# The end of a graph layer on one core: the last four row tiles as two rounds of two through the same ring memory

## The chip, the core and the metric

The kernel runs on one core of a Trainium2 chip. The metric is the device time of one execution in microseconds (us). Matmuls run on PE (TensorE), copies and square roots on ACT (ScalarE), everything elementwise on DVE (VectorE). SP (SyncE) only issues DMAs; ACT issues three small ones.

## What is computed

One layer of a graph network with residual and layer norm, all in float32, with x of 8192 x 64, adj of 8192 x 8192 (268 MB, stored dense), w of 8192 and W of 64 x 64:

```python
agg = adj @ (x @ W_agg)
y = x + w[:, None] * relu(agg) + (1.0 - w)[:, None] * x
out = (y - mean(y)) / sqrt(var(y) + 1e-5)      # over the 64 columns
```

## The kernel before

The 8192 rows of the output are 64 row tiles of 128 rows. The kernel computes (adj @ x) @ W, so that W comes in only at the end of each group of tiles. For one group of n tiles it contracts over 64 blocks of 128 rows of x: block j is `x_sb[:, j]` (128 x 64) as the stationary operand and 128 x (n·128) numbers of the transposed matrix as the moving one. Even blocks add up in PSUM partitions 0 to 63, odd ones in 64 to 127. The host has laid the matrix out so that a load of some blocks is one run of memory per partition.

There are 15 main groups of four tiles (512 columns), then a group of three ("mid", 384 columns) and a group of one ("last", 128 columns). Each main group comes in three loads of 22, 22 and 20 blocks (5.77, 5.77 and 5.24 MB), which go to the three slots of `ring`. The mid group comes in eight loads (`MID_LOADS`), the last group in nine (`LAST_LOADS`); mid starts at the beginning of `ring`, last lies behind it, in the third slot.

SP issues all loads on one queue, in the order of the program. A main load waits on `slot_free` until PE has consumed what stood in its slot three loads ago (L119 to L123). The mid loads wait for as many slots as they reach into (L126 to L132), the last loads for the third slot (L133). After them SP waits until 63 tiles are done and stores them (2 MB, L140 and L141); ACT stores the last tile (L214).

PE (L167 to L187) waits for each load on the load's own semaphore and contracts it (`contract`, L156). When a group is complete, ACT copies the sums from PSUM to `aggT` (L203, L208, L211) and PE turns them back (`turn_back`, L164): one matmul per tile, with `aggT` stationary and W, stacked twice, moving, which also adds the even and odd halves. Then DVE does the rest: `weigh` (L245) and `normalise` (L234 to L242) for the groups of four and three tiles, with ACT's square root (L199) in between. The group of one tile has a shorter chain of its own with `bn_stats` and `bn_aggr` (L261 to L267). Each DVE step waits for the one before it. A program's matmul in fp32 appears in the profile as two MATMULs, so 22 blocks are 44 of them.

Of the kernel before, what the change touches and what calls it, by code (L numbers as in the profile page):

```python
# [4 lines left out]
P = 128  # L5
D = 64
EPS = 1e-5
HALVES = 1
MAIN_SLOTS = 4
MID_SLOTS = 3  # L10
LAST_SLOTS = 1
SUB = 64
MAIN_LOADS = (22, 22, 20)
MID_LOADS = (16, 12, 12, 8, 8, 4, 2, 2)
LAST_LOADS = (10, 12, 12, 10, 7, 5, 4, 2, 2)


def gnn_residual_layernorm(nc, x, adj_main, adj_mid, adj_last, w, w_agg, out):

# [10 lines left out]
    ALU = mybir.AluOpType  # L30
# [2 lines left out]

    T = x.shape[0] // P
    G = adj_main.shape[0]
    MID, LAST = G, G + 1
    MID_T0 = G * MAIN_SLOTS
    LAST_T0 = MID_T0 + MID_SLOTS
    COLS, MID_COLS = MAIN_SLOTS * P, MID_SLOTS * P
    C = len(MAIN_LOADS)  # L40
    SLOT = max(MAIN_LOADS) * COLS
    LAST_AT = T * MID_COLS
    assert SUB == T == sum(MAIN_LOADS) == sum(MID_LOADS) == sum(LAST_LOADS) and LAST_T0 + LAST_SLOTS == T
    assert LAST_AT + T * P <= C * SLOT and LAST_AT > (C - 1) * SLOT


    DVE_PRE = 2
    DVE_GROUP, VAR_STEP = 7, 6
    LAST_STEP0 = DVE_PRE + LAST * DVE_GROUP
    LAST_VAR_STEP = 4  # L50

    ctx = ExitStack()
    with ctx:
        def sb(name, shape):
            return ctx.enter_context(nc.sbuf_tensor(name, shape, fp32))
# [4 lines left out]
        def sem(name):  # L60
            return ctx.enter_context(nc.semaphore(name))
# [5 lines left out]
        two_minus_w = sb("two_minus_w", [P, T])  # L67
        wagg2 = sb("wagg2", [P, D])
        eps = sb("eps", [P, 1])
        aggT = sb("aggT", [P, COLS])  # L70
        y = sb("y", [P, MAIN_SLOTS, D])
        sq = sb("sq", [P, MAIN_SLOTS, D])
# [1 line left out]
        varsum = sb("varsum", [P, MAIN_SLOTS])  # L74
        std = sb("std", [P, MAIN_SLOTS])
        rstd = sb("rstd", [P, MAIN_SLOTS])
        y_last = sb("y_last", [P, D])
        rstd_last = sb("rstd_last", [P, 1])
        std_last = sb("std_last", [P, 1])
        stats = sb("stats", [P, 6])  # L80
        mv = sb("mv", [P, 2])

        bank = psum("bank", [P, 8, 512])
        acc = bank[:, 0]
        mid_acc = bank[:, 1, 0:MID_COLS]
        last_acc = bank[:, 2, 0:P]
        rows_ps = bank[:, 3, 0:MAIN_SLOTS * D]
        mid_rows = bank[:, 4, 0:MID_SLOTS * D]
        last_rows = bank[:, 5, 0:D]

        loaded = [sem(f"loaded{c}") for c in range(C)]
        mid_loaded = [sem(f"mid_loaded{k}") for k in range(len(MID_LOADS))]
        last_loaded = [sem(f"last_loaded{k}") for k in range(len(LAST_LOADS))]
# [3 lines left out]
        mid_done, last_done = sem("mid_done"), sem("last_done")  # L97
        agg_copied = sem("agg_copied")
        rows_done = sem("rows_done")
        dve_step = sem("dve_step")  # L100
# [6 lines left out]
        @block.sync  # L107
        def _(sp):
            sp.dma_start(x_sb[:], x.rearrange("(p t) d -> p t d", p=P)).then_inc(x_in, 16)  # L109
            sp.dma_start(w_sb[:], w.rearrange("(p t) -> p t", p=P)).then_inc(w_in, 16)  # L110
            def main_load(c, load):

                j, n = sum(MAIN_LOADS[:c]), MAIN_LOADS[c]
                sp.dma_start(ring[:, c * SLOT:c * SLOT + n * COLS], load[:, :, j:j + n].rearrange("o q s n -> (o q) (s n)")  # L114
                             ).then_inc(loaded[c], 16)

            for c in range(C):
                main_load(c, adj_main[0:1, 0])
            with sp.Fori(1, G) as g:  # L119
                for c in range(C):  # L120

                    sp.wait_ge(slot_free, g * C + (c + 1 - C))
                    main_load(c, adj_main[bass.ds(g, 1), 0])  # L123

            j, freed = 0, 0
            for k, n in enumerate(MID_LOADS):  # L126
                while freed * SLOT < (j + n) * MID_COLS:
                    freed += 1
                    sp.wait_ge(slot_free, (G - 1) * C + freed)
                sp.dma_start(ring[:, j * MID_COLS:(j + n) * MID_COLS],  # L130
                             adj_mid[0, :, j:j + n].rearrange("q s n -> q (s n)")).then_inc(mid_loaded[k], 16)
                j += n  # L132
            sp.wait_ge(slot_free, G * C)  # L133
            j = 0
            for k, n in enumerate(LAST_LOADS):
                sp.dma_start(ring[:, LAST_AT + j * P:LAST_AT + (j + n) * P],
                             adj_last[:, j:j + n].rearrange("q s n -> q (s n)")).then_inc(last_loaded[k], 16)
                j += n

            sp.wait_ge(out_ready, LAST)  # L140
            sp.dma_start(out_rows[:, 0:LAST_T0], res[:, 0:LAST_T0]).then_inc(stored, 16)  # L141

        @block.gpsimd
        def _(pool):
            nc.gpsimd.memset(eps[:], EPS).then_inc(eps_ready, 1)

        @block.tensor
        def _(pe):
            pe.wait_ge(x_in, 16)
            pe.wait_ge(wagg_in, 32)  # L150

            def contract(into, at, cols, j0, n):

                for s in range(n):
                    j = j0 + s
                    last = nc.tensor.matmul(into[j % 2 * D:(j % 2 + 1) * D, 0:cols], x_sb[:, j],  # L156
                                            ring[:, at + s * cols:at + (s + 1) * cols], start=j < 2, stop=j >= T - 2)
                return last

            def turn_back(rows, n, copied):  # L160

                pe.wait_ge(agg_copied, copied)
                for i in range(n):
                    last = nc.tensor.matmul(rows[:, i * D:(i + 1) * D], aggT[:, i * P:(i + 1) * P], wagg2[:], start=True, stop=True)  # L164
                last.then_inc(rows_done, 1)

            with pe.Fori(0, G) as g:  # L167
                for c in range(C):
                    pe.wait_ge(loaded[c], g * 16 + 16)
                    contract(acc, c * SLOT, COLS, sum(MAIN_LOADS[:c]), MAIN_LOADS[c]).then_inc(slot_free, 1)  # L170

                pe.wait_ge(dve_step, g * DVE_GROUP + DVE_PRE)
                turn_back(rows_ps, MAIN_SLOTS, g + 1)
            j = 0
            for k, n in enumerate(MID_LOADS):
                pe.wait_ge(mid_loaded[k], 16)
                last = contract(mid_acc, j * MID_COLS, MID_COLS, j, n)
                j += n
            last.then_inc(mid_done, 1)
            turn_back(mid_rows, MID_SLOTS, MID + 1)  # L180
            j = 0
            for k, n in enumerate(LAST_LOADS):
                pe.wait_ge(last_loaded[k], 16)
                last = contract(last_acc, LAST_AT + j * P, P, j, n)
                j += n
            last.then_inc(last_done, 1)
            turn_back(last_rows, LAST_SLOTS, LAST + 1)  # L187

        @block.scalar
        def _(act):  # L190
# [10 lines left out]
            with act.Fori(0, G) as g:  # L201
# [5 lines left out]
            act.wait_ge(mid_done, 1)  # L207
            nc.scalar.copy(aggT[:, 0:MID_COLS], mid_acc).then_inc(agg_copied, 1)  # L208
            std_of(std[:, 0:MID_SLOTS], varsum[:, 0:MID_SLOTS], 1.0 / D, MID * DVE_GROUP + (DVE_PRE + VAR_STEP))
            act.wait_ge(last_done, 1)  # L210
            nc.scalar.copy(aggT[:, 0:P], last_acc).then_inc(agg_copied, 1)  # L211
            std_of(std_last[:], mv[:, 1:2], 1.0, LAST_STEP0 + LAST_VAR_STEP)
# [5 lines left out]
        def _(dve):  # L218
            def step(instruction, count):
                instruction.then_inc(dve_step, 1)  # L220
                dve.wait_ge(dve_step, count)
# [32 lines left out]
            base = MID * DVE_GROUP + DVE_PRE  # L254
            dve.wait_ge(rows_done, MID + 1)
            weigh(mid_rows, MID_T0, MID_SLOTS, base)
            normalise(MID, MID_T0, MID_SLOTS, base)

            v, t = y_last[:], LAST_T0
            dve.wait_ge(rows_done, LAST + 1)  # L260
            step(nc.vector.tensor_scalar(v, last_rows, 0.0, w_sb[:, t:t + 1], ALU.max, ALU.mult), LAST_STEP0 + 1)  # L261
            step(nc.vector.tensor_tensor(v, v, res[:, t], ALU.add), LAST_STEP0 + 2)  # L262
            step(nc.vector.bn_stats(stats[:], v), LAST_STEP0 + 3)  # L263
            step(nc.vector.bn_aggr(mv[:], stats[:]), LAST_STEP0 + LAST_VAR_STEP)  # L264
            dve.wait_ge(std_ready, LAST + 1)
            step(nc.vector.reciprocal(rstd_last[:], std_last[:]), LAST_STEP0 + 5)
            nc.vector.tensor_scalar(res[:, t], v, mv[:, 0:1], rstd_last[:, 0:1], ALU.subtract, ALU.mult).then_inc(out_ready, 1)  # L267


# [31 lines left out]
```

## Time and profile before

| | |
|---|---|
| three runs | 638.78, 640.0, 640.12 us, median 640.0 |
| the profiled execution | 638.89 us, its span in the trace 637.0 us |
| mean granted clock of TensorE | 0.912 of full speed |
| bytes moved by DMA | 272.75 MB, mean 428 GB/s |
| busy | PE 82%, DVE 9%, ACT 2% of the span |

The span is what the trace covers; the time of the execution is 1.9 us longer. Times in the trace count from the start of the span.

### The profile page before, as it was taken

The page shows a single profiled execution, that of the slowest core. Times are in us where ns is not written, and L with a number is a line of the kernel's source. Part 1 is how long each engine was busy: PE and PEld are TensorE (multiplying, and loading weights), DVE is VectorE, ACT ScalarE, POOL GpSimd, SP SyncE. Part 2 cuts the span into 40 slices and gives each one's busy share as a digit, 9 for nine tenths or more (in the row PEclk, how much of TensorE's full clock was granted, in tenths as well). Part 3 has the DMA queues.
Part 4 walks back from the last instruction along what each step waited for, and adds up shares of the span by engine and source line. Part 5 has one row for each costly group of instructions (what it writes and reads, how often), then busy time and mean ns, then how long its engine had stood idle before and what let it go on. Part 6 is the DMA issues. An engine that isn't in the chain of part 4 may idle for free.

```text
span 637.0 us, 5371 instructions
## 1 busy us (share of the span) xinstructions
PE 519.5 (82%) x2304; PEld 177.2 (28%) x2304; DVE 55.8 (9%) x136; ACT 15.9 (2%) x35; POOL 0.3 (0%) x5
## 2 busy tenths in 40 slices
PE   0678798878987888797878977878887987978996
PEld 0123232222222322222222322322222222222345
DVE  2000101010010100101001010100101001010102
ACT  0000000000000000000000000000000000000000
POOL 0000000000000000000000000000000000000000
PEclk9997898888979889897988979898888989888999
DMA  9999999999999999999999999999999999999998
GB/s 362 453 418 453 419 427 433 425 447 428 444 414 447 419 429 443 441 432 419 451 410 436 436 450 423 427 431 425 446 424 453 424 429 419 436 444 420 428 413 349
DMA packets 9667, 272.75 MB, mean 428 GB/s; under 512 B 1472, under 2 KB 1728, under 8 KB 3008
## 3 DMA queue, kind: packets, MB, share of 16 engines
q1 hardware_dynamic: 9360, 272.63, 99.6%
q10 hardware_dynamic: 304, 0.07, 0.1%
q8 instruction: 3, 0.05, 0.0%
HBM read 270.60 MB, written 2.10 MB: 428 GB/s over the span
## 4 chain that ended last, share of the span: by engine, by line
DMA 69%; PE 29%; issue 0%; SPq 0%; ACT 0%; DVE 0%; DVEq 0%
DMA ring<-adj_main_dram 69%; PE bank L156 29%; PE bank L164 0%; SPq L114 0%; ACT aggT L203 0%; ACT aggT L208 0%; SPq L110 0%; SPq L109 0%; DVE res L267 0%; ACT std_last L199 0%; DVE y_last L261 0%; ACT aggT L211 0%; DVE stats L263 0%; DVE y_last L262 0%; DVE mv L264 0%
## 5 line engine op out<-in xcount | busy, mean ns | idle before, releaser
L156 PE MATMUL bank<-ring,x_sb 128*64 128x512 f32 (+2 forms) x2176 | 501.7, 621 | 102.2 <-DMA ring<-adj_main_dram 102.1
L156 PEld LDWEIGHTS bank<-ring,x_sb 128*64 128x64 f32 x2176 | 161.6, 148 | 430.2 <-issue 299.7
L245 DVE SCALAR_TENSOR_TENSOR y<-bank,w_sb 128x256 f32<-128x256 f32 (+1 forms) x16 | 6.7, 420 | 552.7 <-PE bank L164 552.7
L164 PE MATMUL bank<-wagg,aggT 128*128 128x64 f32 x128 | 17.9, 281 | 11.2 <-ACT aggT L203 10.3
L164 PEld LDWEIGHTS bank<-wagg,aggT 128*128 128x128 f32 x128 | 15.6, 191 | 25.4 <-ACT aggT L203 23.5
L203 ACT COPY aggT<-bank 128x512 f32<-128x512 f32 x15 | 8.8, 585 | 527.0 <-PE bank L156 527.0
L234 DVE TENSOR_TENSOR y<-y,res 128x256 f32<-128x256 f32 (+1 forms) x16 | 6.7, 420 | 2.2
L242 DVE TENSOR_TENSOR res<-y,rstd 128x256 f32 (+1 forms) x16 | 6.7, 421 | 0.6
L238 DVE TENSOR_TENSOR sq<-y 128x256 f32<-128x256 f32 (+1 forms) x16 | 6.7, 421 | 0.6
L236 DVE SCALAR_TENSOR_TENSOR y<-rowsum,y 128x256 f32<-128x256 f32 (+1 forms) x16 | 6.7, 420 | 0.5
L239 DVE TENSOR_REDUCE varsum<-sq 128x4 f32<-128x256 f32 (+1 forms) x16 | 6.7, 416 | 0.5
L235 DVE TENSOR_REDUCE rowsum<-y 128x4 f32<-128x256 f32 (+1 forms) x16 | 6.6, 416 | 0.6
L199 ACT ACTIVATE std<-varsum,eps 128x4 f32<-128x4 f32 (+1 forms) x16 | 4.8, 297 | 65.7 <-DVE varsum L239 65.7
L230 DVE TENSOR_TENSOR res<-x_sb,two_minus_w 128x4096 f32<-128x4096 f32 x1 | 4.4, 4425 | 0.0
L241 DVE RECIPROCAL rstd<-std 128x4 f32<-128x4 f32 (+1 forms) x16 | 2.8, 178 | 6.9 <-ACT std L199 6.9
L194 ACT ACT_TABLE_LOAD x1 | 1.3, 1283 | 2.0 <-issue 2.0
L227 DVE TENSOR_SCALAR two_minus_w<-w_sb 128x64 f32<-128x64 f32 x1 | 0.2, 194 | 9.2 <-DMA w_sb<-w_dram 9.2
L208 ACT COPY aggT<-bank 128x384 f32<-128x384 f32 x1 | 0.5, 478 | 17.5 <-PE bank L156 17.5
L261 DVE TENSOR_SCALAR y_last<-bank,w_sb 128x64 f32<-128x64 f32 x1 | 0.3, 284 | 4.8 <-PE bank L164 4.8
L211 ACT COPY aggT<-bank 128x128 f32<-128x128 f32 x1 | 0.3, 265 | 4.7 <-PE bank L156 4.7
L199 ACT ACTIVATE std_last<-mv,eps 128x1 f32<-128x1 f32 x1 | 0.3, 296 | 1.6 <-DVE mv L264 1.6
L267 DVE TENSOR_SCALAR res<-y_last,mv,rstd_last 128x64 f32<-128x64 f32 x1 | 0.3, 314 | 0.0
(9 smaller groups left out, 1.3 us busy)
## 6 DMA issues: line engine op xcount, KB each, us to landing
ring<-adj_main_dram SPq DMA_DIRECT2D x30, 5632.0 KB, 27.2
ring<-adj_main_dram SPq DMA_DIRECT2D x15, 5120.0 KB, 29.8
ring<-adj_mid_dram SPq DMA_DIRECT2D x2, 2304.0 KB, 22.8
ring<-adj_mid_dram SPq DMA_DIRECT2D x1, 3072.0 KB, 21.5
ring<-adj_mid_dram SPq DMA_DIRECT2D x2, 1536.0 KB, 23.9
x_sb<-x_dram SPq DMA_DIRECT2D x1, 2048.0 KB, 8.0
out_dram<-res SPq DMA_DIRECT2D x1, 2016.0 KB, 8.1
ring<-adj_last_dram SPq DMA_DIRECT2D x2, 768.0 KB, 23.0
```

What stands on the lines that cost most here:

```text
L156: last = nc.tensor.matmul(into[j % 2 * D:(j % 2 + 1) * D, 0:cols], x_sb[:, j], ring[:, at + s * cols:at + (s + 1) * cols], start=j < 2, st ...
L164: last = nc.tensor.matmul(rows[:, i * D:(i + 1) * D], aggT[:, i * P:(i + 1) * P], wagg2[:], start=True, stop=True)
L199: nc.scalar.activation(out_std, var, ACT.Sqrt, bias=eps[:, 0:1], scale=scale).then_inc(std_ready, 1)
L203: nc.scalar.copy(aggT[:], acc).then_inc(agg_copied, 1)
L230: step(nc.vector.tensor_tensor(res[:], x_sb[:], over_row(two_minus_w[:]), ALU.mult), DVE_PRE)
L234: step(nc.vector.tensor_tensor(v, v, residual, ALU.add), base + 2)
L235: step(nc.vector.tensor_reduce(rowsum[:, 0:n], v, AX.X, ALU.add), base + 3)
L236: step(nc.vector.scalar_tensor_tensor(out=v, in0=over_row(rowsum[:, 0:n]), scalar=-1.0 / D, in1=v, op0=ALU.mult, op1=ALU.add), base + 4)
L238: step(nc.vector.tensor_tensor(s, v, v, ALU.mult), base + 5)
L239: step(nc.vector.tensor_reduce(varsum[:, 0:n], s, AX.X, ALU.add), base + VAR_STEP)
L242: nc.vector.tensor_tensor(residual, v, over_row(rstd[:, 0:n]), ALU.mult).then_inc(out_ready, 1)
L245: step(nc.vector.scalar_tensor_tensor(out=y[:, 0:n], in0=rows.rearrange("p (n d) -> p n d", d=D), scalar=0.0, in1=over_row(w_sb[:, bass.ds ...
```

## The change

The last four tiles become two groups of two ("pairs", 256 columns each), and both go through one loop body.

- The host arrays keep their names: `adj_mid` now holds tiles 60 and 61, `adj_last` tiles 62 and 63.
- A pair comes in seven loads of 20, 15, 11, 8, 5, 3 and 2 blocks. Both rounds use the same place, the first 64 x 256 columns of `ring`, which reach into the second slot. Load k of round one waits for the slots, load k of round two for `pair_free` to reach k + 1, which PE counts up behind each contracted piece.
- PE runs both rounds in one `Fori(0, 2)`. ACT copies a pair tile by tile, and each matmul of turning back waits for its own copy.
- DVE runs `weigh` and `normalise` on two tiles in both rounds; the shorter chain for one tile is gone. Before each round DVE waits for `out_ready` of its previous group.
- The last load (20 blocks) of the last main group is issued as two of 10. PE waits for the second half on `rest_loaded` in all 15 passes, at a value from a register: 1 in the first 14 (a memset on POOL counts it up at the start) and 17 in the last.
- The first store now covers 62 tiles, the second two tiles (64 KB).

```diff
+PAIR_LOADS = (20, 15, 11, 8, 5, 3, 2)
+REST = 10
...
-            with sp.Fori(1, G) as g:
+            with sp.Fori(1, G - 1) as g:
...
+            for c in range(C):
+                sp.wait_ge(slot_free, (G - 1) * C + (c + 1 - C))
+                whole = MAIN_LOADS[c] - (REST if c == C - 1 else 0)
+                main_load(c, adj_main[G - 1:G, 0], 0, whole, loaded[c])
+            main_load(C - 1, adj_main[G - 1:G, 0], whole, whole + REST, rest_loaded)
+            def pair_load(k, group):
+                j, n = sum(PAIR_LOADS[:k]), PAIR_LOADS[k]
+                sp.dma_start(ring[:, j * PAIR_COLS:(j + n) * PAIR_COLS], group[:, j:j + n].rearrange("q s n -> q (s n)")
+                             ).then_inc(pair_loaded[k], 16)
+            freed = 0
+            for k in range(K):
+                while freed * SLOT < sum(PAIR_LOADS[:k + 1]) * PAIR_COLS:
                     freed += 1
                     sp.wait_ge(slot_free, (G - 1) * C + freed)
+                pair_load(k, adj_mid[0])
+            for k in range(K):
+                sp.wait_ge(pair_free, k + 1)
+                pair_load(k, adj_last)
...
+                    if c < C - 1:
+                        last = contract(acc, c * SLOT, COLS, j, n)
+                    else:
+                        whole = n - REST
+                        contract(acc, c * SLOT, COLS, j, whole)
+                        pe.wait_ge(rest_loaded, (g + (16 - (G - 1))) // 16 * 16 + 1)
+                        last = contract(acc, c * SLOT + whole * COLS, COLS, j + whole, REST)
+                    last.then_inc(slot_free, 1)
...
+            with pe.Fori(0, 2) as r:
+                j = 0
+                for k, n in enumerate(PAIR_LOADS):
+                    pe.wait_ge(pair_loaded[k], r * 16 + 16)
+                    contract(pair_acc, j * PAIR_COLS, PAIR_COLS, j, n).then_inc(pair_free, 1)
+                    j += n
+                for i in range(PAIR):
+                    pe.wait_ge(agg_copied, r * PAIR + (G + i + 1))
+                    last = nc.tensor.matmul(pair_rows[:, i * D:(i + 1) * D], aggT[:, i * P:(i + 1) * P], wagg2[:], start=True, stop=True)
+                last.then_inc(rows_done, 1)
...
+            for r in range(2):
+                act.wait_ge(pair_free, (r + 1) * K)
+                for i in range(PAIR):
+                    nc.scalar.copy(aggT[:, i * P:(i + 1) * P], pair_acc[:, i * P:(i + 1) * P]).then_inc(agg_copied, 1)
+                std_of(std[:, 0:PAIR], varsum[:, 0:PAIR], 1.0 / D, (G + r) * DVE_GROUP + (DVE_PRE + VAR_STEP))
...
+            for r in range(2):
+                base, t0 = (G + r) * DVE_GROUP + DVE_PRE, PAIR_T0 + r * PAIR
+                dve.wait_ge(out_ready, G + r)
+                dve.wait_ge(rows_done, G + r + 1)
+                weigh(pair_rows, t0, PAIR, base)
+                normalise(G + r, t0, PAIR, base)
```

SP's queue behind the last main load, before the change (the sizes are numbers per partition; 384 columns of a mid block, 128 of a last one):

```order
L130 DMA ring<-adj_mid_dram 128x768 x2
L136 DMA ring<-adj_last_dram 128x1280 [waits slot_free]
L136 DMA ring<-adj_last_dram 128x1536 x2
L136 DMA ring<-adj_last_dram 128x1280
L136 DMA ring<-adj_last_dram 128x896
L136 DMA ring<-adj_last_dram 128x640
L136 DMA ring<-adj_last_dram 128x512
L136 DMA ring<-adj_last_dram 128x256 x2
L141 DMA out_dram<-res 128x4032 [waits out_ready]
```

The loads of the last group wait once, for a slot. The same place after the change:

```order
L126 DMA ring<-adj_mid_dram 128x512
L126 DMA ring<-adj_last_dram 128x5120 [waits pair_free]
L126 DMA ring<-adj_last_dram 128x3840 [waits pair_free]
L126 DMA ring<-adj_last_dram 128x2816 [waits pair_free]
L126 DMA ring<-adj_last_dram 128x2048 [waits pair_free]
L126 DMA ring<-adj_last_dram 128x1280 [waits pair_free]
L126 DMA ring<-adj_last_dram 128x768 [waits pair_free]
L126 DMA ring<-adj_last_dram 128x512 [waits pair_free]
L142 DMA out_dram<-res 128x3968 [waits out_ready]
```

Every load of the second round now waits for PE, and the big store stands behind all of them as before.

DVE at the end of the program, before the change: the group of three tiles, then the chain of the single tile.

```order
L242 TENSOR_TENSOR res<-y,rstd 128x192
L261 TENSOR_SCALAR y_last<-bank,w_sb 128x64
L262 TENSOR_TENSOR y_last<-y_last,res 128x64
L263 BN_STATS stats<-y_last 128x6
L264 BN_AGGR mv<-stats 128x2
L266 RECIPROCAL rstd_last<-std_last 128x1
L267 TENSOR_SCALAR res<-y_last,mv,rstd_last 128x64
```

And after it, the end of round one and round two:

```order
L250 TENSOR_TENSOR res<-y,rstd 128x128
L253 SCALAR_TENSOR_TENSOR y<-bank,w_sb 128x128
L242 TENSOR_TENSOR y<-y,res 128x128
L243 TENSOR_REDUCE rowsum<-y 128x2
L244 SCALAR_TENSOR_TENSOR y<-rowsum,y 128x128
L246 TENSOR_TENSOR sq<-y 128x128
L247 TENSOR_REDUCE varsum<-sq 128x2
L249 RECIPROCAL rstd<-std 128x2
L250 TENSOR_TENSOR res<-y,rstd 128x128
```

Six operations on 64 numbers per partition have become eight, on 128.

## Rows read from the trace of the kernel before

**Rows 1.** The page: span, and busy tenths of PE and the DMA engines.
```profile
span 637.0 us, 5371 instructions
PE 519.5 (82%) x2304; PEld 177.2 (28%) x2304; DVE 55.8 (9%) x136; ACT 15.9 (2%) x35; POOL 0.3 (0%) x5
DMA  9999999999999999999999999999999999999998
```
**Rows 2.** The page: the chain of work that ended last, by engine.
```profile
DMA 69%; PE 29%; issue 0%; SPq 0%; ACT 0%; DVE 0%; DVEq 0%
```
**Rows 3.** Timeline: start us, us, engine line op out<-in xcount [idle before <-releaser].
```profile
579.82 11.36 PE L156 MATMUL bank<-ring,x_sb 128*64 128x512 f32 x44 [2.12 <-DMA ring<-adj_main_dram]
...
591.95 8.80 PE L156 MATMUL bank<-ring,x_sb 128*64 128x512 f32 x40 [0.77 <-DMA ring<-adj_main_dram]
...
602.48 20.86 PE L156 MATMUL bank<-ring,x_sb 128*64 128x384 f32 x128
```
**Rows 4.** SP's last issues in the timeline, and the same by size and us to landing.
```profile
601.64 0.43 SPq L130 DMA_DIRECT2D ring<-adj_mid_dram  x1
ring<-adj_mid_dram SPq DMA_DIRECT2D x1, 384.0 KB, 19.8
617.46 0.79 SPq L136 DMA_DIRECT2D ring<-adj_last_dram  x1
ring<-adj_last_dram SPq DMA_DIRECT2D x1, 128.0 KB, 14.1
628.18 0.34 SPq L141 DMA_DIRECT2D out_dram<-res  x1
out_dram<-res SPq DMA_DIRECT2D x1, 2016.0 KB, 8.1
```
**Rows 5.** Timeline of the end; the final row is ACT's store in the list of DMA issues.
```profile
624.73 7.38 PE L156 MATMUL bank<-ring,x_sb 128*64 128x128 f32 x128
632.16 0.27 ACT L211 COPY aggT<-bank 128x128 f32<-128x128 f32 x1 [4.68 <-PE bank L156]
632.95 0.28 DVE L261 TENSOR_SCALAR y_last<-bank,w_sb 128x64 f32<-128x64 f32 x1 [4.80 <-PE bank L164]
634.61 0.31 DVE L267 TENSOR_SCALAR res<-y_last,mv,rstd_last 128x64 f32<-128x64 f32 x1
634.95 0.35 ACTq L214 DMA_DIRECT2D out_dram<-res  x1
out_dram<-res ACTq DMA_DIRECT2D x1, 32.0 KB, 1.7
```
**Rows 6.** Stretches: us, busy (xcount) of PE, PEld, DVE, ACT, POOL; PEclk, DMA share, GB/s.
```profile
566.49:569.90 3.41, 3.41 (x10) 1.09 (x12) 0.83 (x3) 0.30 (x1) 0.00 (x0) 0.54 0.98 423
633.50:634.50 1.00, 0.00 (x0) 0.00 (x0) 0.51 (x3) 0.30 (x1) 0.00 (x0) 1.00 0.50 210
634.50:635.50 1.00, 0.00 (x0) 0.00 (x0) 0.38 (x2) 0.00 (x0) 0.00 (x0) 0.50 0.23 97
631.55:637.00 5.45, 1.00 (x14) 0.62 (x8) 1.40 (x6) 0.56 (x2) 0.00 (x0) 0.77 0.53 216
```
**Rows 7.** Timeline of PE: main loads contracted after waits of different length.
```profile
35.36 9.66 PE L156 MATMUL bank<-ring,x_sb 128*64 128x512 f32 x44 [1.25 <-DMA ring<-adj_main_dram]
217.42 11.36 PE L156 MATMUL bank<-ring,x_sb 128*64 128x512 f32 x44 [1.03 <-DMA ring<-adj_main_dram]
463.46 11.36 PE L156 MATMUL bank<-ring,x_sb 128*64 128x512 f32 x44 [1.97 <-DMA ring<-adj_main_dram]
```
**Rows 8.** Mean ns by shape, then the end of the three-tile group in the timeline.
```profile
L242 DVE TENSOR_TENSOR res<-y,rstd 128x256 f32 x15 | 6.4, 425 | 0.5
L242 DVE TENSOR_TENSOR res<-y,rstd 128x192 f32<-128x192 f32 x1 | 0.4, 357 | 0.0
627.18 0.30 ACT L199 ACTIVATE std<-varsum,eps 128x3 f32<-128x3 f32 x1 [3.32 <-DVE varsum L239]
627.58 0.18 DVE L241 RECIPROCAL rstd<-std 128x3 f32<-128x3 f32 x1 [0.43 <-ACT std L199]
627.79 0.36 DVE L242 TENSOR_TENSOR res<-y,rstd 128x192 f32<-128x192 f32 x1
```

More of the change, by code:

```diff
@@ L9 @@
 MAIN_SLOTS = 4
-MID_SLOTS = 3
-LAST_SLOTS = 1
+MID_SLOTS = 2
+LAST_SLOTS = 2
 SUB = 64
 MAIN_LOADS = (22, 22, 20)
-MID_LOADS = (16, 12, 12, 8, 8, 4, 2, 2)
-LAST_LOADS = (10, 12, 12, 10, 7, 5, 4, 2, 2)
+PAIR_LOADS = (20, 15, 11, 8, 5, 3, 2)
+REST = 10
 def gnn_residual_layernorm(nc, x, adj_main, adj_mid, adj_last, w, w_agg, out):
@@ L35, in gnn_residual_layernorm @@
     G = adj_main.shape[0]
[L36 to L39, printed above, removed]
+    LAST = G + 1
+    PAIR = MID_SLOTS
+    PAIR_T0 = G * MAIN_SLOTS
+    LAST_T0 = PAIR_T0 + PAIR
+    COLS, PAIR_COLS = MAIN_SLOTS * P, PAIR * P
     C = len(MAIN_LOADS)
     SLOT = max(MAIN_LOADS) * COLS
-    LAST_AT = T * MID_COLS
-    assert SUB == T == sum(MAIN_LOADS) == sum(MID_LOADS) == sum(LAST_LOADS) and LAST_T0 + LAST_SLOTS == T
-    assert LAST_AT + T * P <= C * SLOT and LAST_AT > (C - 1) * SLOT
+    K = len(PAIR_LOADS)
+    assert G <= 16 and SUB == T == sum(MAIN_LOADS) == sum(PAIR_LOADS) and LAST_T0 + LAST_SLOTS == T and PAIR == LAST_SLOTS
+    assert T * PAIR_COLS <= C * SLOT
     DVE_PRE = 2
     DVE_GROUP, VAR_STEP = 7, 6
-    LAST_STEP0 = DVE_PRE + LAST * DVE_GROUP
-    LAST_VAR_STEP = 4
     ctx = ExitStack()
@@ L69, in gnn_residual_layernorm @@
         eps = sb("eps", [P, 1])
+        one = sb("one", [P, 1])
         aggT = sb("aggT", [P, COLS])
@@ L76, in gnn_residual_layernorm @@
         rstd = sb("rstd", [P, MAIN_SLOTS])
[L77 to L81, printed above, removed]
         bank = psum("bank", [P, 8, 512])
         acc = bank[:, 0]
[L85 to L89, printed above, removed]
+        pair_acc = bank[:, 1, 0:PAIR_COLS]
+        rows_ps = bank[:, 2, 0:MAIN_SLOTS * D]
+        pair_rows = bank[:, 3, 0:PAIR * D]
         loaded = [sem(f"loaded{c}") for c in range(C)]
-        mid_loaded = [sem(f"mid_loaded{k}") for k in range(len(MID_LOADS))]
-        last_loaded = [sem(f"last_loaded{k}") for k in range(len(LAST_LOADS))]
+        rest_loaded = sem("rest_loaded")
+        pair_loaded = [sem(f"pair_loaded{k}") for k in range(K)]
+        pair_free = sem("pair_free")
         slot_free = sem("slot_free")
@@ L96, in gnn_residual_layernorm @@
         eps_ready = sem("eps_ready")
-        mid_done, last_done = sem("mid_done"), sem("last_done")
         agg_copied = sem("agg_copied")
@@ L110, in _, with main_load @@
             sp.dma_start(w_sb[:], w.rearrange("(p t) -> p t", p=P)).then_inc(w_in, 16)
[L111 to L115, printed above, removed]
+            def main_load(c, load, first, end, landed):
+                j, at = sum(MAIN_LOADS[:c]), c * SLOT
+                sp.dma_start(ring[:, at + first * COLS:at + end * COLS],
+                             load[:, :, j + first:j + end].rearrange("o q s n -> (o q) (s n)")).then_inc(landed, 16)
@@ L117, in _ @@
             for c in range(C):
-                main_load(c, adj_main[0:1, 0])
-            with sp.Fori(1, G) as g:
+                main_load(c, adj_main[0:1, 0], 0, MAIN_LOADS[c], loaded[c])
+            with sp.Fori(1, G - 1) as g:
                 for c in range(C):
                     sp.wait_ge(slot_free, g * C + (c + 1 - C))
[L123 to L127, printed above, removed]
+                    main_load(c, adj_main[bass.ds(g, 1), 0], 0, MAIN_LOADS[c], loaded[c])
@@ L128, in _ @@
+            freed = 0
+            for k in range(K):
+                while freed * SLOT < sum(PAIR_LOADS[:k + 1]) * PAIR_COLS:
                     freed += 1
                     sp.wait_ge(slot_free, (G - 1) * C + freed)
[L130 to L138, printed above, removed]
+                pair_load(k, adj_mid[0])
@@ L145, in _ @@
             nc.gpsimd.memset(eps[:], EPS).then_inc(eps_ready, 1)
+            nc.gpsimd.memset(one[:], 1.0).then_inc(rest_loaded, 1)
         @block.tensor
@@ L169, in _ @@
                     pe.wait_ge(loaded[c], g * 16 + 16)
-                    contract(acc, c * SLOT, COLS, sum(MAIN_LOADS[:c]), MAIN_LOADS[c]).then_inc(slot_free, 1)
+                    j, n = sum(MAIN_LOADS[:c]), MAIN_LOADS[c]
+                    if c < C - 1:
[6 more added lines that the diff above has]
+                    last.then_inc(slot_free, 1)
                 pe.wait_ge(dve_step, g * DVE_GROUP + DVE_PRE)
                 turn_back(rows_ps, MAIN_SLOTS, g + 1)
[L174 to L187, printed above, removed]
+            with pe.Fori(0, 2) as r:
[8 more added lines that the diff above has]
+                last.then_inc(rows_done, 1)
         @block.scalar
@@ L206, in _ @@
                 act.wait_ge(out_ready, g + 1)
[L207 to L212, printed above, removed]
+            for r in range(2):
[3 more added lines that the diff above has]
+                std_of(std[:, 0:PAIR], varsum[:, 0:PAIR], 1.0 / D, (G + r) * DVE_GROUP + (DVE_PRE + VAR_STEP))
             act.wait_ge(out_ready, LAST + 1)
@@ L252, in _ @@
                 normalise(g, g * MAIN_SLOTS, MAIN_SLOTS, base)
[L254 to L267, printed above, removed]
+            for r in range(2):
[4 more added lines that the diff above has]
+                normalise(G + r, t0, PAIR, base)
 def kernel(x, adj, L0_gnn_w, L0_gnn_W_agg):
```

## The prediction

> **What bounds the kernel now.** I read the page first, then the DMA issues with their times to landing, then the timeline of the end, and last the stretches. The reader should see in the page that all 16 DMA engines are busy in practically every slice, while PE is busy 82% of the span and every other engine far less [rows 1]. The chain that ended last says the same: 69% of it is a wait for the matrix and 29% is PE consuming it [rows 2]. So the body of the kernel costs what its bytes cost, and the change leaves the bytes alone. Only the end can differ: when does the last load land, and how much work follows it?
>
> The timeline gives the fixed point. The last load of the last main group lands at 591.95, where PE starts on it [rows 3]. Behind it, 16.78 MB of matrix are left (64 blocks x 128 rows x 512 columns x 4 bytes). The last of these loads is issued at 617.46 and lands 14.1 us later, at 631.56 [rows 4]. That is 39.6 us, or 424 GB/s. The 2 MB store is issued at 628.18 and lands 8.1 us later, at 636.3 [rows 4]; that is 4.7 us behind the last load, the time of 2.06 MB at 435 GB/s. So the queue serves in order: the store waits behind the loads and doesn't slow them. After the last landing, PE ends at 632.11, ACT copies, PE turns one tile back, DVE normalises until 634.92, and the final 32 KB store, issued at 634.95, lands 1.7 us later, at 636.65 [rows 5]. Everything after 631.56 is a serial tail of 5.1 us, and it runs with the DMA engines at 53% [rows 6]. The change rebuilds just this tail.
>
> **The change, part by part.**
>
> *The last load of the last main group in halves.* PE finishes the load before it at 591.18 (579.82 + 11.36) and then idles 0.77 until 591.95 [rows 3]. Ten blocks are now there earlier, so PE starts at 591.2 and finishes at about 599.8 instead of 600.75. PE is 0.95 us earlier into the tail groups, at 601.5 instead of 602.48 [rows 3]. That is slack, not time: the loads set the end. In the 15 passes the added wait on a register costs PE some register work beside DMA waits of 0.77 us and more: nothing.
>
> *Bytes and loads.* After 591.95, 17 loads become 14. At 432 GB/s, the pace of the main loads (5.24 MB from 579.82 to 591.95 [rows 3]), 16.78 MB take 38.8 us; the 17 loads took 39.6, so I put 0.045 us on each. Fourteen, and one more main load, save 0.09 us: last landing 631.47.
>
> *Two rounds through one ring memory.* Load k of round two may be issued only when PE has consumed piece k of round one. Is PE in time? One block takes PE 20.86 us / 64 = 0.326 at 384 columns [rows 3] and 7.38 / 64 = 0.115 at 128 [rows 5]; at 256 I take 0.215, two thirds of 0.326 without the drain at its end. PE frees the first piece at 601.5 + 20 x 0.215 = 605.8 and the seventh at 615.4. Round one's loads end at 591.95 + 8.39 MB / 0.425 = 611.7. So the first load of round two (2.6 MB, 6.1 us of work) is queued 5.9 us before the queue would run dry, the other six by 615.4, before that first one has landed at 617.8. The queue never empties. Cost nothing; the cover is those 5.9 us.
>
> *PE at the end.* The pieces of round two land at 617.8, 622.4, 625.8, 628.3, 629.8, 630.8 and 631.47. From the fourth on, 18 blocks x 0.215 = 3.9 us follow 628.35, so PE ends at 632.23 instead of 632.11: +0.12.
>
> *Copy and turning back.* Before: 0.79 us from the start of the copy (632.16) to DVE (632.95) [rows 5]. Now two copies of 128 columns follow each other and the second matmul waits for the second copy. The first matmul is hidden behind the second copy, so one copy of 0.27 and its gap are added: +0.29.
>
> *Normalising two tiles with seven steps in place of one with six.* An operation takes 425 ns on 256 elements and 357 on 192 [rows 8], so about 290 on 128; with the gap of 34 ns of the 192-wide run a step is 0.325. Six steps make 1.95. From the square root to the reciprocal it takes 0.40 (627.18 to 627.58), from there to the last operation 0.21 (to 627.79) [rows 8], and that operation 0.29: 2.85 in all, against 634.92 - 632.95 = 1.97 [rows 5]: +0.88. DVE's new wait for its own previous group is met long before.
>
> *The stores.* The first (62 tiles) is issued near 620 but stands behind all loads, and lands at 636.2, near where it lands now; the second is issued at about 636.2, so the first no longer matters. The last store is 64 KB instead of 32. The trace has no 64 KB store. By the 32 KB one it is 1.7 us [rows 5]; from below I allow 1.4, since the big store has just left the engines, from above 2.2. I take 1.7, the nearest row: 0.
>
> The sum is 0.12 + 0.29 + 0.88 = 1.29; the 0.09 of the earlier landing is already in the 632.23. The profiled execution took 638.89, so it would become 640.2. It lies low among the runs: with the three (638.78, 640.0, 640.12) the mean is 639.4, and the forecast for a median of runs is 640.7.
>
> One rule speaks for the other sign. Loads under 1 MiB: twelve of the last 17 before, six of 14 now. The last 4.19 MB, in nine such loads, came between 621.4 (where the last load of the three-tile group, issued at 601.64, landed after 19.8 us) and 631.56 [rows 4]: 413 GB/s, only 4% under the main loads. The Trainium skill, "DMA: Bandwidth & Descriptors", section Bandwidth, asks for DMAs of at least 1 MiB for 75% of the peak. By that rule the small loads would have been some 2.4 us dearer than the new ones, and the change would be faster by about 1.1 us; the row above disagrees, because loads queued behind each other hide their fixed part here.
>
> **The rivals.**
>
> *PE's clock falls before round two* (35%, slower). After round one PE turns two tiles back (until 616.4) and then waits for the first piece at 617.8, about 1.4 us. Waits of 1.97 us before a main load were followed by the 1.2 GHz level: 11.36 us for 22 blocks; waits of 1.03 to 1.25 us were followed by it three times in eight (11.36 against 9.66 us) [rows 7]. In the 3.4 us after such a wait the mean granted clock was 0.54 [rows 6]. 1.4 us lies between. It would cost 1.7 us on the first piece; PE, with 64 blocks to do in the 13.7 us up to the last landing, couldn't catch up: 617.8 + 1.7 + 13.76 = 633.27, so 1.04 us later. Time 641.7. It decides if the PE clock shows 1.2 GHz after 617.8. For it speaks also that PE has had idle time around the copies; against it, five of eight.
>
> *The leading DMA engines run dry, and the slow ones gain* (9%, faster). After 631.56 the DMA share is 0.50 from 633.5 on and 0.23 from 634.5 [rows 6], though the last store lands only at 636.3. So some engines finish 2 to 3 us before the last, and a landing is set by the slowest. If round two's gate starved the leaders and gave their share to the others, the last load could land up to 2.5 us earlier: 639.4 + 1.3 - 2.5 = 638.2. This needs the leaders, who end round one near 609, to find nothing: but the next load is issued at 605.8, and 1.7 us is what even a whole small store takes to land. So I think it unlikely.
>
> *The gate itself holds the queue* (4%, slower). If PE freed the first piece after 610, a gap would open, and each us adds one: 641.7 with 1 us. The 5.9 us speak against it, even after a slow stretch of 1.7.
>
> *Large loads count for more than I say* (5%, faster). If the price per load grows as its rows shrink, all of the 0.8 us of the 17 loads could vanish, which moves the last landing and all behind it: 639.4 + 1.29 - 0.7 = 640.0. By the rule of the page it would be 1.29 - 2.4 on 639.4, so 638.3.
>
> **How the numbers follow.** The forecast case (47%): full clock, queue full, a tail longer by 1.29 us. Its own range is 0.9 to 1.8 with the bounds of the last store. Timings of this kernel tell a difference of about 0.2%, 1.28 us, from none; so this case is half "same", half "slower". The slow-clock case is slower but for a seventh of it. The two faster cases give 9% faster and the rest same. Together: faster 0.09, same 0.34, slower 0.57. The range takes in the clock case with its spread of runs, (641.7 + 0.8) and below the forecast the spread of the runs, 0.6, and part of the large-load case: 639.2 to 642.7.
>
> **What would show it.** Last load landing within 0.5 us of 631.5; PE's last contraction ending near 632.2 at 2.4 GHz; 1.05 us from there to DVE; DVE's last group 2.85 us; last store issued near 636.2 and the span near 638.3. A DMA share well under 1 between 606 and 631 would show the gate; half clock after 617.8 the first rival; a landing before 631 either of the faster ones. The prediction is wrong if the last load lands over 0.7 us off, since all the rest of the sum hangs on it.

## The result and the profile after

The changed kernel took 641.32 us in the median of 8 runs (640.31 to 642.38), the kernel before 639.92 in 8 (638.69 to 640.17). The ratio is 1.0031 with a 95% interval of 1.0022 to 1.0040: slower by 1.4 to 2.6 us. The two medians differ by 1.40 us, the lower end of that; the runs of both kernels fall into groups, so a median moves with the share of each group. The profiled execution took 640.31, the lowest of the eight, with a span of 638.5; against the 638.89 of the one before that is +1.42.

The page shows the same picture as before [rows 1, 2], with the last slices of the DMA engines a little emptier:

```profile
span 638.5 us, 5392 instructions
PE 519.5 (81%) x2304; PEld 180.8 (28%) x2304; DVE 56.1 (9%) x138; ACT 16.0 (3%) x37; POOL 0.3 (0%) x6
DMA  9999999999999999999999999999999999999997
...
DMA 69%; PE 29%; issue 0%; DVE 0%; SPq 0%; ACT 0%; DVEq 0%
```

The end in the timeline (start us, us, engine line op out<-in xcount [idle before <-releaser]), which answers to [rows 5]; the last row is from the list of DMA issues:

```profile
617.85 14.67 PE L159 MATMUL bank<-ring,x_sb 128*64 128x256 f32 x128 [0.47 <-DMA ring<-adj_last_dram]
632.55 0.43 ACT L219 COPY aggT<-bank 128x128 f32<-128x128 f32 x2 [12.83 <-PE bank L159]
632.87 0.66 PE L195 MATMUL bank<-wagg,aggT 128*128 128x64 f32 x4 [0.35 <-ACT aggT L219]
633.64 0.29 DVE L253 SCALAR_TENSOR_TENSOR y<-bank,w_sb 128x128 f32<-128x128 f32 x1 [13.33 <-PE bank L195]
...
635.58 0.30 ACT L208 ACTIVATE std<-varsum,eps 128x2 f32<-128x2 f32 x1 [2.60 <-DVE varsum L247]
...
636.18 0.29 DVE L250 TENSOR_TENSOR res<-y,rstd 128x128 f32<-128x128 f32 x1
636.50 0.35 ACTq L222 DMA_DIRECT2D out_dram<-res  x1
...
out_dram<-res ACTq DMA_DIRECT2D x1, 64.0 KB, 1.6
```

The reader should see one thread from PE to the last store without a hole: PE ends at 632.52 (617.85 + 14.67), DVE starts 1.09 us after the start of the copies, works 2.83 us, and the store is issued at 636.50 and lands at 638.1.

The gate of round two, in SP's issues, and the landing of loads and of the big store, which answer to [rows 4]. Above the list of issues stands the stretch 634 to 635 (us, busy of PE, PEld, DVE, ACT, POOL, PEclk, DMA share, GB/s), which answers to [rows 6]:

```profile
606.89 9.89 SPq L126 DMA_DIRECT2D ring<-adj_last_dram  x7
620.34 0.34 SPq L142 DMA_DIRECT2D out_dram<-res  x1
...
634.00:635.00 1.00, 0.00 (x0) 0.00 (x0) 0.90 (x4) 0.00 (x0) 0.00 (x0) 1.00 0.08 32
...
ring<-adj_last_dram SPq DMA_DIRECT2D x1, 2560.0 KB, 10.9
out_dram<-res SPq DMA_DIRECT2D x1, 1984.0 KB, 15.8
...
ring<-adj_last_dram SPq DMA_DIRECT2D x1, 256.0 KB, 15.0
```

The first load of round two is issued at 606.89 and lands at 617.8. The last one is issued within 0.1 us of 616.4 and lands 15.0 us later, at 631.4: where the last load landed before (631.56). The big store lands at 636.1. Before, it ended 0.3 us ahead of the last store, so the tail cost little beyond the DMA work that had to be done anyway; now the engines are at 8% in the stretch from 634 to 635, where before the change they were at 50% from 633.5 and at 23% from 634.5 [rows 6], and the end of the tail stands almost alone.

### The profile page after: what moved, and what is told of

It is laid out like the page before. It is cut to its first block, busy times and chain, and to the rows that moved or that the text cites. A ratio compares the mean times of both kernels' runs of the same rounds, so it can differ in the third digit from the quotient of the medians.

```text
span 638.5 us, 5392 instructions
## 1 busy us (share of the span) xinstructions
PE 519.5 (81%) x2304; PEld 180.8 (28%) x2304; DVE 56.1 (9%) x138; ACT 16.0 (3%) x37; POOL 0.3 (0%) x6
## 4 chain that ended last, share of the span: by engine, by line
DMA 69%; PE 29%; issue 0%; DVE 0%; SPq 0%; ACT 0%; DVEq 0%
DMA ring<-adj_main_dram 67%; PE bank L159 29%; DMA ring<-adj_last_dram 2%; SPq L109 0%; PE bank L167 0%; PE bank L195 0%; ACT aggT L212 0%; SPq L105 0%; SPq L104 0%; ACT std L208 0%; DVE sq L246 0%; DVE y L242 0%; DVE y L244 0%; DVE y L253 0%; DVE varsum L247 0%
## 5 line engine op out<-in xcount | busy, mean ns | idle before, releaser
L159 PE MATMUL bank<-ring,x_sb 128*64 128x512 f32 (+1 forms) x2176 | 501.7, 621 | 103.0 <-DMA ring<-adj_main_dram 102.5
L159 PEld LDWEIGHTS bank<-ring,x_sb 128*64 128x64 f32 x2176 | 165.3, 148 | 427.4 <-issue 289.0
```

## The experiments

My theory: the longer serial tail behind an unchanged last landing is the cost in the profiled execution (1.42 us), and what the median has on top is PE's clock, which falls in some executions before round two. Against it stand the gate on PE's consumption, a later landing, and PE's backlog.

The runs of the kernel before that were taken beside the experiments are 29, 23, 21 and 1. They lie in two groups, 638.4 to 639.05 and 639.4 to 640.3, half of them (37 of 74) in the upper one. The medians of the first three sets are 639.46, 638.97 and 638.95, though the groups stay where they are: the median falls into one group or the other. So the runs of a changed kernel are best compared with the groups, and ratios of different sets with care.

### Round two in memory of its own

```diff
-                sp.dma_start(ring[:, j * PAIR_COLS:(j + n) * PAIR_COLS], ...
+                sp.dma_start(ring[:, (r * T + j) * PAIR_COLS:(r * T + j + n) * PAIR_COLS], ...
...
+            sp.wait_ge(slot_free, G * C)
             for k in range(K):
-                sp.wait_ge(pair_free, k + 1)
-                pair_load(k, adj_last)
+                pair_load(k, adj_last, 1)
...
-            with pe.Fori(0, 2) as r:
+            for r in range(2):
```

> The changed kernel, with round two of the pairs in ring memory of its own and both rounds written out, so that no load waits for PE within the pairs. If the longer work behind the last landing is the whole cost (my theory): the same as the changed kernel, 641.3 (ratio to before 1.002 to 1.003), last landing near 631.5. If the gate on PE's consumption holds the queue or skews the DMA engines: the last load lands earlier by what it cost, so 640.0 or less. If it helped (leading engines held back), the last load lands later and the time rises over 642.

Measured: median 642.15 of 6 runs (640.18 to 642.50), ratio 1.0033 (1.0020 to 1.0046). Without the gate it isn't faster. The profiled execution was one of the longer ones (642.37). SP issued its last load at 605.90, 10 us earlier than with the gate, and it landed at the same time:

```profile
605.90 1.16 SPq L126 DMA_DIRECT2D ring<-adj_last_dram  x1
...
ring<-adj_last_dram SPq DMA_DIRECT2D x1, 256.0 KB, 25.6
```

605.90 + 25.6 = 631.5. In the stretches of this trace the DMA engines are busy throughout (0.96 and 0.99 of the time from 617.95 to 624). So neither the gate nor the early end of some DMA engines moves the last landing. What did move is PE:

```profile
614.00 0.66 PE L194 MATMUL bank<-wagg,aggT 128*128 128x64 f32 x4 [0.36 <-ACT aggT L218]
617.95 16.59 PE L158 MATMUL bank<-ring,x_sb 128*64 128x256 f32 x128 [3.29 <-DMA ring<-adj_last_dram]
...
617.95:621.40 3.45, 3.45 (x16) 1.95 (x18) 0.00 (x0) 0.00 (x0) 0.00 (x0) 0.50 0.96 408
```

PE had waited 3.29 us before round two, ran at first at 0.50 of its clock, that is 1.2 GHz, and took 16.59 us for it instead of 14.67.

### The last main load whole again

```diff
-                whole = MAIN_LOADS[c] - (REST if c == C - 1 else 0)
-                main_load(c, adj_main[G - 1:G, 0], 0, whole, loaded[c])
-            main_load(C - 1, adj_main[G - 1:G, 0], whole, whole + REST, rest_loaded)
+                main_load(c, adj_main[G - 1:G, 0], 0, MAIN_LOADS[c], loaded[c])
...
+                    contract(acc, c * SLOT, COLS, j, n).then_inc(slot_free, 1)
```

> The changed kernel with the last load of the last main group whole again. My theory: this load is not on the path once round two starts by its landing (617.8), so the same within 0.3 us of the changed kernel. Rival, PE's backlog: PE starts round one up to 1 us later, frees round two's pieces later and ends later, up to 1 us slower. Second rival, PE's clock: with less waiting before round two (under 0.5 us) there is no fall to 1.2 GHz, and runs that had it lose their tail: faster by up to 1 us in the median.

Measured: median 641.03 of 12 runs, ratio 1.0031 (1.0019 to 1.0043). By the median this is the first reading, 0.29 us from the 641.32 of the changed kernel. But the runs are spread otherwise: two clean groups, six between 639.90 and 640.26, six between 641.79 and 642.85, where the changed kernel had one of eight in the lower group and most between 641.1 and 641.5. The profiled execution (640.13) is of the lower one:

```profile
591.75 8.80 PE L157 MATMUL bank<-ring,x_sb 128*64 128x512 f32 x40 [0.77 <-DMA ring<-adj_main_dram]
617.67 14.67 PE L157 MATMUL bank<-ring,x_sb 128*64 128x256 f32 x128 [0.34 <-DMA ring<-adj_last_dram]
```

With the load whole, PE starts on it only when all of it has landed, at 591.75, takes 8.80 us at full clock, and so has but 0.34 us left to wait before round two. A run in which PE comes later has less still. So the upper group of this kernel can't be a fall of the clock after a long wait before round two; PE coming late, after a fall in the last main load or in round one, would fit, and no trace shows it. So the half load seems to take one kind of longer run away and to bring another, which is argued and not shown.

### The kernel before with the seven-step chain

```diff
-            step(nc.vector.tensor_scalar(v, last_rows, 0.0, w_sb[:, t:t + 1], ALU.max, ALU.mult), LAST_STEP0 + 1)
...
+            weigh(last_rows, LAST_T0, LAST_SLOTS, base)
+            normalise(LAST, LAST_T0, LAST_SLOTS, base)
```

> The kernel before, with the last single tile normalised by the general seven steps in place of the shorter chain. At 64 elements a step is 0.224 + 0.034 us: 6 x 0.258 + 0.40 + 0.21 + 0.22 = 2.4 us against 1.97: if the chain behind the last landing is on the path, slower by 0.4 us (ratio 1.0007). If the big store or the last landing on the slow DMA engines sets the end, 0.

Measured: median 639.09 of 11 runs, ratio 1.0002 (0.9993 to 1.0011). By the medians this is inconclusive: 0.4 us is less than the distance between the two groups of runs. Group by group both lie higher: the seven lower runs have a median of 638.99 for 638.81 in the kernel before, the four upper ones 640.35 for 639.95. The chain in the profile:

```profile
633.10 0.23 DVE L245 SCALAR_TENSOR_TENSOR y<-bank,w_sb 128x64 f32<-128x64 f32 x1 [5.02 <-PE bank L164]
635.24 0.23 DVE L242 TENSOR_TENSOR res<-y,rstd 128x64 f32<-128x64 f32 x1
```

It goes from 633.10 to 635.47, 2.37 us for the 1.97 of before, and the span is 637.4 for 637.0.

### The kernel before with the split main load

```diff
+            for c in range(C):
+                sp.wait_ge(slot_free, (G - 1) * C + (c + 1 - C))
+                whole = MAIN_LOADS[c] - (REST if c == C - 1 else 0)
+                main_load(c, adj_main[G - 1:G, 0], 0, whole, loaded[c])
+            main_load(C - 1, adj_main[G - 1:G, 0], whole, whole + REST, rest_loaded)
...
+                        pe.wait_ge(rest_loaded, (g + (16 - (G - 1))) // 16 * 16 + 1)
+                        last = contract(acc, c * SLOT + whole * COLS, COLS, j + whole, REST)
```

> The kernel before, with the last load of the last main group in two halves and nothing else. There PE works without a pause from 624.73 to 632.11 and ends 0.56 us behind the last landing. If PE's backlog is part of its end: PE ends within 0.25 us of the landing, so 0.3 us faster in the profile, and more in the runs near 640.0, which may be those in which PE's clock fell in the last main group: median 638.9. If the landing alone sets the end: the same as before, median 639.9.

Measured: median 638.82 of 11 runs, all between 638.62 and 639.19; ratio 0.9988 (0.9980 to 0.9997). This is faster than the changed kernel, and against the kernel before it is faster by having no upper group: its median is that of the lower group (638.81). The group near 640 is gone. But the mechanism that I gave for the profile is wrong: PE ended at 632.22, not earlier than before, 0.54 us behind the last landing (617.48 + 14.2 = 631.68). The timeline shows why this isn't backlog: PE now has waits in the mid group.

```profile
579.47 18.25 PE L166 MATMUL bank<-ring,x_sb 128*64 128x512 f32 x84 [3.66 <-DMA ring<-adj_main_dram]
...
599.43 9.25 PE L166 MATMUL bank<-ring,x_sb 128*64 128x384 f32 x56
609.97 6.67 PE L166 MATMUL bank<-ring,x_sb 128*64 128x384 f32 x40 [1.29 <-DMA ring<-adj_mid_dram]
...
632.27 0.27 ACT L230 COPY aggT<-bank 128x128 f32<-128x128 f32 x1 [4.98 <-PE bank L166]
```

PE comes 3 us earlier to the mid group than in [rows 3]: some 0.8 us because it needn't wait for the whole last load, and 1.9 because its clock didn't fall in this execution (18.25 us for the 42 blocks that took 11.36 + 8.80 there). It could have ended earlier if its own work had held it; it follows the loads, half a microsecond behind. That the upper group of the kernel before is PE coming late after a fall of its clock in the last main group fits with this, and was not seen in a trace.

### Filling PE's wait before round two

```diff
                 last.then_inc(rows_done, 1)
+                for f in range(6):
+                    nc.tensor.matmul(bank[f % 2 * D:(f % 2 + 1) * D, 4, 0:PAIR_COLS], x_sb[:, f],
+                                     x_sb[:, 0:4].rearrange("p t d -> p (t d)"), start=True, stop=True)
```

> The changed kernel, with PE contracting 6 blocks (256 columns, 1.3 us) of x with itself into an unused PSUM bank behind each turning back of a pair; nobody reads them. Clock theory: the runs over 641 are those in which PE waited 1 to 3.3 us before round two and then ran at 1.2 GHz. With half or more of that wait filled, most of them go: median 640.2 to 640.8. Rival, the spread comes from the landing of the loads or from elsewhere: 641.0 to 641.4 and two groups of runs as before. Cost of the filler where the wait was only 0.5 us: up to 0.3 us, since PE catches up on the loads.

> The same with 12 blocks (2.6 us). Clock theory: no run of the slow group is left, all within 0.5 us of one another; PE starts round two up to 2.1 us after the first landing in the runs in which it had waited least, which costs these up to 1 us; median 640.3 to 641.2. Rival as in the run with 6: two groups, distance 2 us.

Measured, with 6: median 640.27 of 11 runs, all between 640.12 and 640.55, ratio 1.0018 (1.0009 to 1.0027). With 12: median 640.42 of 12 runs (640.06 to 640.86, and one of 641.83), ratio 1.0020 (1.0011 to 1.0028). Work that nobody reads makes the changed kernel faster by about 1 us in the median (641.32 without it) and, with 6 blocks, takes away every run over 640.6. With 12 blocks "all within 0.5 us" did not come true: the runs spread over 0.8 us, and the one of 641.83 has no trace. The timeline with 6 blocks:

```profile
614.59 1.51 PE L198 MATMUL bank<-x_sb 128*64 128x256 f32 x12
617.78 14.68 PE L159 MATMUL bank<-ring,x_sb 128*64 128x256 f32 x128 [1.68 <-DMA ring<-adj_last_dram]
```

PE turned the first pair back at the same time as in the run with its own memory (614.00 in both), which had 3.29 us to wait and lost its clock; with 1.68 us left to wait it kept it. The price of filling too much shows with 12:

```profile
616.43 2.81 PE L198 MATMUL bank<-x_sb 128*64 128x256 f32 x24
619.07 13.98 PE L159 MATMUL bank<-ring,x_sb 128*64 128x256 f32 x128
```

PE worked on the filling until it started round two at 619.07, 1.3 us after the first load, and ended at 633.05; that run took 640.86.

### Two steps less behind the last landing

On top of the kernel with 6 filling blocks:

```diff
+                if short:
+                    base -= 2
+                else:
                     step(nc.vector.tensor_tensor(v, v, residual, ALU.add), base + 2)
                     step(nc.vector.tensor_reduce(rowsum[:, 0:n], v, AX.X, ALU.add), base + 3)
...
+                normalise(G + r, t0, PAIR, base, short=r == 1)
```

> The kernel with 6 filling blocks (640.27), and in the second round of the pairs DVE leaves out two of its steps: adding the residual, and the row sum (so tiles 62 and 63 lack the residual and use the row sums of tiles 60 and 61). If the serial work behind the last landing sets the end: faster by two steps of 0.324 us, 0.65 us, median 639.6. If the big store on the slow DMA engines or the last landing set it by now (they end near 636.1 in the trace, 2 us before the last store): less than 0.3.

Measured: median 639.58 of 11 runs (639.34 to 639.91), 0.69 us under the same kernel with both steps (640.27), where 0.65 was expected. The two groups of eleven runs don't overlap. Serial work behind the last landing goes into the time in full, although the big store is still under way for part of it.

### One copy in place of two

```diff
-                for i in range(PAIR):
-                    nc.scalar.copy(aggT[:, i * P:(i + 1) * P], pair_acc[:, i * P:(i + 1) * P]).then_inc(agg_copied, 1)
+                nc.scalar.copy(aggT[:, 0:PAIR_COLS], pair_acc).then_inc(agg_copied, PAIR)
```

> The kernel with 6 filling blocks, with one copy of 256 columns in place of two of 128. The two overlap in the trace (0.43 us together) and the first matmul hides behind the second copy. One copy of 256 columns should take 0.37 us (0.27 for 128, 0.48 for 384, 0.59 for 512), and both of PE's turns then follow it, 0.22 us more behind the copy: from the start of the copy to DVE 1.09 + (0.37 - 0.43) + 0.1 = 1.1 to 1.2. Time the same, 640.3 within 0.15. My forecast had counted the second copy at its full 0.27; if the copies didn't overlap, one copy would be 0.15 faster.

Measured: median 640.42 of 11 runs (ten between 640.22 and 640.56, one of 1031.67, which is out of line with all others); no difference beyond the 0.15 us that was allowed for. The copies as one, in the timeline:

```profile
632.53 0.37 ACT L221 COPY aggT<-bank 128x256 f32<-128x256 f32 x1 [13.64 <-PE bank L159]
632.95 0.66 PE L195 MATMUL bank<-wagg,aggT 128*128 128x64 f32 x4 [0.52 <-ACT aggT L221]
633.72 0.29 DVE L255 SCALAR_TENSOR_TENSOR y<-bank,w_sb 128x128 f32<-128x128 f32 x1 [14.24 <-PE bank L195]
```

1.19 us from copy to DVE, for 1.09 with two copies: in the traces, copying tile by tile is worth 0.1 us, and the times (640.42 for 640.27) don't contradict it.

### More executions of the two kernels as they are

> The changed kernel unchanged, for one more profiled execution (the one there is took 640.31; most runs took 641.1 to 641.5). If this one lies over 641: clock theory, PE's wait before round two is over 0.5 us, a stretch of 3.4 us at the start of round two is at 1.2 GHz in part or whole, and PE ends 0.5 to 2 us later than 632.5 with the last landing still at 631.5. Rival: the last landing itself is later.

> The changed kernel once more, for a second profiled execution, with the two readings of the look before: either PE's clock at the start of round two, or a later last landing.

> The kernel before unchanged, once more profiled (its runs lie in two groups, near 638.7 and near 639.9). If it is one near 639.9: by my theory PE's clock falls at the second or third load of the last main group, PE comes to the mid group over 0.5 us later than 602.48, works without a pause and ends 1 us later than 632.11, with the last landing at 631.5. Rival: the last landing is later. If it is one near 638.7 it says nothing.

Measured: 642.48, 640.10 and, for the kernel before, 638.84. The first two are the same program. The longer one, in the timeline and in the stretches from the start of round two on:

```profile
614.11 0.66 PE L195 MATMUL bank<-wagg,aggT 128*128 128x64 f32 x4 [0.36 <-ACT aggT L219]
617.93 16.74 PE L159 MATMUL bank<-ring,x_sb 128*64 128x256 f32 x128 [3.16 <-DMA ring<-adj_last_dram]
...
617.98:621.40 3.42, 3.42 (x17) 1.90 (x19) 0.00 (x0) 0.00 (x0) 0.00 (x0) 0.50 0.96 409
621.40:624.00 2.60, 2.60 (x18) 1.53 (x16) 0.00 (x0) 0.00 (x0) 0.00 (x0) 0.60 1.00 421
...
613.79 0.40 SPq L126 DMA_DIRECT2D ring<-adj_last_dram  x1
ring<-adj_last_dram SPq DMA_DIRECT2D x1, 256.0 KB, 17.7
```

and the shorter one:

```profile
615.47 0.66 PE L195 MATMUL bank<-wagg,aggT 128*128 128x64 f32 x4 [0.37 <-ACT aggT L219]
617.64 14.67 PE L159 MATMUL bank<-ring,x_sb 128*64 128x256 f32 x128 [1.52 <-DMA ring<-adj_last_dram]
```

The last load of the longer one lands at 613.79 + 17.7 = 631.5, as in the profiled execution (631.4). PE waits 3.16 us, contracts round two at half clock at first, and the copies begin at 634.72 instead of 632.35. That is 2.37 us, and the times differ by 2.38. The kernel before fell into its lower group again, so its upper one stays without a trace.

Why the wait differs shows one step earlier. PE's last 42 blocks of the last main group, in the profiled execution of the result, in the shorter one here and in the longer one:

```profile
579.76 20.83 PE L159 MATMUL bank<-ring,x_sb 128*64 128x512 f32 x84 [3.67 <-DMA ring<-adj_main_dram]
579.55 19.80 PE L159 MATMUL bank<-ring,x_sb 128*64 128x512 f32 x84 [2.28 <-DMA ring<-adj_main_dram]
579.75 18.25 PE L159 MATMUL bank<-ring,x_sb 128*64 128x512 f32 x84 [0.79 <-DMA ring<-adj_main_dram]
```

18.25 us is the time at full clock. Where the clock fell here, PE came later to the pairs and had little to wait before round two (0.47 and 1.52 us); where it didn't, PE came early, waited 3.16 us, and the clock fell then, where it costs time.

## Why the prediction was right

**The sum.** It named an unchanged last landing and three terms of the tail, 1.29 us together, and 640.2 for the profiled execution; that took 640.31.

| step | forecast | measured |
|---|---|---|
| last landing | 631.47 | 631.4 |
| first piece of round two lands | 617.8 | 617.8 |
| PE ends | 632.23 (+0.12) | 632.52 (+0.41) |
| copy to DVE | 1.08 (+0.29) | 1.09 (+0.30) |
| DVE's chain | 2.85 (+0.88) | 2.83 (+0.86) |
| last store | 1.7 (0) | 1.6 (-0.1) |

The terms measured sum to 1.47, for 1.42 in the times. The one that was mis-sized is PE's end, by 0.29 us. A block of 256 columns takes 0.219 us (14.03 us for the 64 of round one, in which PE doesn't wait), not 0.215; over the last 18 blocks that is 0.07. The other 0.2 no row explains. A small delay at each late piece would fit, as in the kernel before with the split, where PE ends half a microsecond behind the last landing without any backlog. My split of the turning back was off though its sum held: the copies overlap (0.43 for both, not 0.54) and the four matmuls take 0.66, not 0.43.

**The queue.** "The queue never empties" held: PE freed the first piece at 606.9, 1.1 us later than I had it, the cover was 4.8 us (up to the 611.7 of the forecast), and the run without the gate landed its last load at the same 631.5. That also speaks against the rival of the leading engines and that of the gate. The store behind the loads did not delay them: issued at 620.34, 8 us earlier than before, and the landing stayed. The Trainium skill, "DMA: Bandwidth & Descriptors", section Queues, rings and completion order, says that each DMA engine takes the descriptors of one queue in order; the trace agrees, with 631.4 against 631.56.

**The number of loads.** The last landing moved by no more than 0.1 to 0.2 us (631.4 against 631.56). That doesn't contradict the 0.045 us per load, but doesn't show it either: in two more profiled executions of the same changed kernel it was at 631.2 and 631.5. The Trainium skill's rule on loads under 1 MiB, "DMA: Bandwidth & Descriptors", section Bandwidth, would by the prediction's estimate have moved it by 2.4 us; here, where loads stand in a queue, the traces don't bear that out.

**The median.** Here the forecast was low: 640.7 against 641.32, inside the range but not by its own case. That it lies in the range is owed to the rival of the falling clock, which the range took in. The two medians differ by 1.40 us where 1.29 was forecast, and that agreement is luck: each median lies about 1 us over the executions that the sum describes (639.92 over the lower group near 638.8, 641.32 over 640.1 to 640.3), the one before for a reason that no trace shows. The step that failed is the choice between the full clock (47%) and the fall (35%). I had worked out PE's wait before round two, 1.4 us, from the one execution in front of me. It isn't a constant. PE ended round one at 616.3, 615.1 and 613.7 in the three traces of this program, because its clock fell more, less or not at all in the last loads of the last main group; so the wait was 0.47, 1.52 and 3.16 us, and only one of the eight timed runs, the profiled one, was near the 640.1 of an undisturbed round two. With the fall PE ended 2.2 us later, not 1.04: round two took 16.74 us where PE needs 14.03 without waits, so the fall cost 2.7 us and not the 1.7 of a main load. The mean clock was still 0.60 from 621.4 to 624; with the stretch before it that makes about 5.5 us of round two at the lower level, half of which is lost. Most of the eight runs (641.1 to 641.5) lie between the two executions that I could see; that they are falls of the clock that began late or ended early fits with the filler, which removed them, but none of them was profiled.

**The half load** in the last main group was costed at nothing ("slack, not time"), and by the median of the changed kernel that held, though the runs without it fall into other groups. It also lets PE come early enough to wait over 3 us before round two: with the load whole the wait was 0.34 us. What I hadn't seen is that the same edit alone takes the upper group away in the kernel before, 0.6 us in the median of that set and less where more of the runs beside it are in the lower group. I read one execution of the lower group and took the spread of the runs, 638.8 to 640.1, for noise.

## What to carry to other kernels

At the end of a kernel that is bound by its loads, find the last landing first, then count only what follows it one by one; each step there entered in full here (two steps of 0.324 us fewer: 0.69 us). A store that must run anyway should hide a tail of its own length and not a longer one; that is argued from the landings (the big store at 636.1 to 636.3 with either tail), and no run here has a tail shorter than the store. When the runs of a kernel fall into groups, the groups are the next thing to explain: a wait of PE that depends on its own history decided here over 2 us. A few matmuls into an unused bank kept the clock through such a wait; of the versions measured the best leaves the tail short and splits only the last main load (638.82 against 639.46 beside it).

## What the runs showed of the hardware

After waits of 3.16 and 3.29 us before round two PE ran at 0.50 of its clock in the first 3.4 us of it, and at a mean of 0.60 and 0.66 in the 2.6 us that followed; after 0.34, 0.47, 1.52 and 1.68 us it did not fall. A longer wait doesn't settle it either way: of three waits of 3.66 to 3.68 us before the second load of the last main group, two were followed by a fall (42 blocks in 20.83 and 20.93 us) and one wasn't (18.25). The issue of a load wasn't what decided its landing in a full queue: the last load landed at 631.2 to 631.7 whether it was issued at 605.9, 613.8, 615.1, 616.4 or 617.5. The big store, issued 8 us earlier behind the same loads, landed at 636.1 for 636.3 and did not delay them.
